# Routed experts of a mixture layer: from dense groups of 16 to a ranking by popularity, with 216 experts in 18 tiles of 12 on 64 token slots

## What is computed

```
h = einsum('btd,pd->btp', x, hasher_w)          # 1024 -> 32
sim = einsum('btp,np->btn', h, keys)            # 256 experts
vals, idx = top_k(sim, 4);  w = softmax(vals)
for k in range(4):
    vd = values_down[idx[..., k]]               # [1024, 32] per row
    vu = values_up[idx[..., k]]                 # [32, 1024] per row
    proj = silu(einsum('btd,btdp->btp', x, vd))
    out += einsum('btp,btpd->btd', proj, vu) * w[..., k:k+1]
return x + out * scale
```

## Time and profile before

| What | us |
|---|---|
| median of three runs | 723.6 |
| span of the profiled execution (first to last instruction) | 720.9 |
| first instruction after the indices of the four experts are known (L1287) | starts at 363.65 |
| one group of 16 experts in the loop | 22.7 |
| end of the last output scaling (L1344) | 718.3 |

### The profile page before, as it was taken

The page is one execution under the profiler, slowest core; times in us unless marked ns, Lnnn a source line. Parts: engine busy times, 40 slices in busy tenths (PEclk is TensorE's granted clock), DMA queues, the critical chain, the costliest instruction groups (busy, mean ns, idle before and its releaser), DMA issues.

```text
span 720.9 us, 9534 instructions
## 1 busy us (share of the span) xinstructions
PE 693.8 (96%) x3308; PEld 544.3 (76%) x3308; DVE 504.1 (70%) x702; ACT 379.9 (53%) x486; POOL 203.2 (28%) x289
## 2 busy tenths in 40 slices
PE   3999999998999999999999999999999999999998
PEld 3877877785555566677878888888888888888886
DVE  5997798599999999677988553464534645356453
ACT  4854989766655656356644534255342543335430
POOL 4038975398489916500500000000000000000000
PEclk9999999999999999999999999999999999999999
DMA  8985332341000006429436536644366444664401
GB/s 307 341 310 221 125 116 88 148 156 78 1 2 1 1 0 243 178 88 340 155 120 241 212 141 218 233 148 181 142 227 233 135 167 163 233 230 127 187 38 60
DMA packets 55177, 114.20 MB, mean 158 GB/s; under 512 B 2245, under 2 KB 35397, under 8 KB 55146
## 3 DMA queue, kind: packets, MB, share of 16 engines
q1 hardware_dynamic: 54538, 112.95, 43.6%
q0 software_dynamic: 160, 0.66, 0.3%
q10 hardware_dynamic: 448, 0.20, 0.1%
HBM read 112.74 MB, written 1.05 MB: 158 GB/s over the span
## 4 chain that ended last, share of the span: by engine, by line
PE 58%; POOL 6%; DVE 5%; issue 5%; ACT 1%; DMA 1%; DVEq 1%; ACTq 0%; POOLq 0%
PE ps L1384 16%; PE ps L1386 16%; PE ps L1385 16%; PE ps L1352 2%; POOL pen L560 2%; POOL oh_src L562 2%; PE ps L1617 2%; POOL pen L567 1%; DVE wlo L870 1%; DVE ps L1057 1%; PE ps L1697 1%; DMA raw<-in_L_gnn_W_on_dram 1%; DVE segmax L1128 1%; PE ps L1678 1%; ACT whi L627 1%
## 5 line engine op out<-in xcount | busy, mean ns | idle before, releaser
L870 DVE TENSOR_TENSOR wlo<-raw,whi 128x2048 fp32r<-128x2048 f32 x99 | 224.4, 2290 | 55.4 <-ACT whi L627 54.7
L627 ACT ACTIVATE whi<-raw 128x2048 fp32r<-128x2048 f32 x104 | 196.3, 1912 | 82.8 <-PE ps L1386 64.8
L1384 PE MATMUL ps<-whi,nT 128*128 128x512 f32 x392 | 157.1, 401 | 0.3 <-ACT act_g L826 0.3
L1386 PE MATMUL ps<-wlo,nT 128*128 128x512 f32 x392 | 153.1, 390 | 0.0
L1385 PE MATMUL ps<-whi,nT 128*128 128x512 f32 x392 | 152.9, 390 | 0.0
L1057 DVE SCALAR_TENSOR_TENSOR ps<-ps,xt 128x1024 f32<-128x1024 f32 x79 | 96.3, 1221 | 1.7 <-PE ps L1410 1.6
L1309 DVE TENSOR_TENSOR gw<-act_g,route 128x512 f32<-128x512 f32 x32 | 20.7, 689 | 105.2 <-ACT act_g L834 105.1
L1384 PE MATMUL ps<-whi,gT_hi 128*128 128x512 f32 x240 | 93.5, 390 | 0.0
L1386 PE MATMUL ps<-wlo,gT_hi 128*128 128x512 f32 x240 | 93.5, 390 | 0.0
L1385 PE MATMUL ps<-whi,gT_lo 128*128 128x512 f32 x240 | 93.4, 389 | 0.0
L1384 PEld LDWEIGHTS ps<-whi,nT 128*128 128x128 f32 x392 | 73.6, 188 | 18.6 <-issue 3.2
(11 more groups left out here) (269 smaller groups left out, 913.4 us busy)
## 6 DMA issues: line engine op xcount, KB each, us to landing
raw<-n_L_ffn_values_down_dram SPq DMA_DIRECT2D x16, 2048.0 KB, 8.2
raw<-in_L_ffn_values_up_dram SPq DMA_DIRECT2D x16, 2048.0 KB, 7.5
raw<-in_L_gnn_W_hh_dram SPq DMA_DIRECT2D x8, 1024.0 KB, 6.1
raw<-in_L_gnn_W_oo_dram SPq DMA_DIRECT2D x8, 1024.0 KB, 6.6
raw<-in_L_gnn_W_ho_dram SPq DMA_DIRECT2D x8, 1024.0 KB, 4.8
raw<-in_L_gnn_W_hn_dram SPq DMA_DIRECT2D x8, 1024.0 KB, 4.8
raw<-in_L_gnn_W_on_dram SPq DMA_DIRECT2D x8, 1024.0 KB, 5.0
xt<-in_x_dram SPq DMA_DIRECT2D x4, 512.0 KB, 7.2
```

What stands on the lines that cost most here:

```text
L627: nc.scalar.activation(half(whi, s, j, down), half(raw, s, j, down), ACT.Copy)\
L870: nc.vector.tensor_tensor(half(wlo, s, j, down), half(raw, s, j, down), half(whi, s, j, down).bitcast(F32), ALU.subtract)\
L1384: nc.tensor.matmul(o, a_hi, b_hi, start=start, stop=False)
L1386: return nc.tensor.matmul(o, a_hi, b_lo, start=False, stop=stop)
```

## The change

Group 0 (experts 0 to 15) stays as it was ("static"). The other 240 experts are ranked by how many tokens chose them. The 24 most chosen ("hot") run dense as before, in 2 groups of 12 (`PER`). The 216 left ("cold") are dealt in turn into 18 tiles (`COLD`) of 12, which run in 9 pairs (`PAIRS`). A tile works on at most 64 tokens (`SLOTS`), those that chose one of its 12 experts: with both parts of x side by side, 64 high and 64 low columns fill the 128 columns of a weight load, and one pass over the high and one over the low part of the matrix gives all products. The rows of x are brought into their slots by matmuls with one-hot matrices (`pick`, by `move_rows`), the routing weights too (`move_weights`), and the results go back to their tokens by matmuls with the turned one-hots (`put`, by `scatter`).

The matrices of a unit (12 experts, down or up, 1.5 MB) are no longer one DMA but 12 of 128 KB, one per expert, at an address that is read from a list of ranks (`by_rank`) into registers of the issuing engine. SP issues the down units, GpSimd the up units. There are three raw buffers of 1.5 MB in a ring (`RAWS`), in which unit n uses buffer n % 3; unit n waits for `lo` of unit n-3 (`raw_free`). A down unit of pair i is number 2+4i+a, an up unit 8+4i+a (the last two 38 and 39), a being 0 or 1.

The loads, as helpers:

```diff
+        def experts(queue, first):
+            return nc.values_load_multi_w_load_instructions(
+                by_rank[0:1, first:first + PER], engines=[queue.engine], min_val=0, max_val=XP - 1,
+                skip_runtime_bounds_check_because="a permutation of the experts, from counted comparisons")[1]
+        def load_down(queue, n, first):
+            down = raw_ring[n % RAWS].rearrange("p (n k) -> p n k", n=PER)
+            for q, e in enumerate(experts(queue, first)):
+                queue.dma_start(down[:, q:q + 1, :], down_v[:, bass.ds(e, 1), :]).then_inc(raw_loaded[n % RAWS], 16)
+        def load_up(queue, n, first):
+            up = raw_ring[n % RAWS].rearrange("p (b d) -> p b d", b=BLK)
+            for q, e in enumerate(experts(queue, first)):
+                at = PD * (q % 4)
+                queue.dma_start(up[at:at + PD, q // 4, :], up_rows[:, bass.ds(e, 1), :].rearrange("w a d -> w (a d)"))\
+                    .then_inc(up_loaded[n % RAWS], 16)
+        def raw_free(queue, n):
+            if n < RAWS:
+                queue.wait_ge(lo_ready[n - 1], 2 * (SLOT_W + 1))
+            else:
+                queue.wait_ge(lo_ready[(n - RAWS) % 2], 2 * turn_of(n - RAWS) + 2)
```

GpSimd's program in this stage (`choose` writes 4 one-hots of 128x64, `write_twice` copies those of a pair, 2 of 128x256; `rows_rest` writes the low part of x, 128x1024):

```diff
+            rows_rest(0)
+            pool.wait_ge(list_ready, 1)
+            raw_free(pool, 2)
+            load_up(pool, 2, 0)
+            pool.wait_ge(taken_ready, 1)
+            choose(0)
+            choose(1)
+            raw_free(pool, 3)
+            load_up(pool, 3, PER)
+            rows_rest(1)
...
+            for pair in range(2, PAIRS):
+                choose(pair)
+            for i in range(PAIRS):
+                write_twice(i)
+                if i:
+                    for a in range(2):
+                        raw_free(pool, up_unit(i - 1, a))
+                        load_up(pool, up_unit(i - 1, a), HOT + (2 * i - 2 + a) * PER)
+            for a in range(2):
+                raw_free(pool, up_unit(PAIRS - 1, a))
+                load_up(pool, up_unit(PAIRS - 1, a), HOT + (2 * PAIRS - 2 + a) * PER)
```

ScalarE's program for pair i (VectorE's has the same order, with `ring_lo`, `add_down`, `cold_weigh`, `sum_lo_part`, `cold_gT_lo` and `x_lo_part` in the places of their partners):

```diff
+                ring_hi(up_unit(i - 1, 0), (0,))
+                send_across(i, 0)
+                ring_hi(up_unit(i - 1, 0), (1,))
+                ring_hi(up_unit(i - 1, 1), (0,))
+                send_across(i, 1)
+                cold_silu(i)
+                sum_hi_part(i - 1, 0, 0)
+                sum_hi_part(i - 1, 0, 1)
+                put_part(i)
+                cold_gT_hi(i)
+                ring_hi(up_unit(i - 1, 1), (1,))
+                ring_hi(after(nxt, 0), (0,))
+                if i < PAIRS - 1:
+                    x_hi_part(i // 2 + 1, 2 * (i % 2))
+                ring_hi(after(nxt, 0), (1,))
+                sum_hi_part(i - 1, 1, 0)
+                sum_hi_part(i - 1, 1, 1)
+                if i < PAIRS - 1:
+                    x_hi_part(i // 2 + 1, 2 * (i % 2) + 1)
+                ring_hi(after(nxt, 1))
```

```diff
+            turn_static()
...
+            up_static()
...
+            hot_down(0)
...
+            hot_turn(0)
+            pe.wait_ge(silu_ready, 2)
+            hot_down(1)
+            pe.wait_ge(gTlo_ready, 2)
+            move_weights(0)
+            hot_up(0)
...
+            hot_turn(1)
...
+            move_rows(0, 0)
+            hot_up(1, lambda b: move_rows(0, b + 1))
+
+            for i in range(PAIRS):
+                cold_down(i, 0)
+                if i >= 2:
+                    scatter(i - 2, 1)
+                cold_down(i, 1)
+                if i:
+                    cold_up(i - 1, 0)
+                else:
+                    move_weights(1)
+                turn_picks(i)
+                cold_turn(i)
+                if i:
+                    scatter(i - 1, 0)
+                if i < PAIRS - 1:
+                    pe.wait_ge(gTlo_ready, 3 + i + 1)
+                    pe.wait_ge(put_ready, i + 1)
+                    move_rows(i // 2 + 1, 2 * (i % 2))
+                if i:
+                    cold_up(i - 1, 1)
+                if i < PAIRS - 1:
+                    move_rows(i // 2 + 1, 2 * (i % 2) + 1)
```

More of the change, by code:

```diff
@@ L83 @@
 GX = 16
-NG = XP // GX
 UNIT = 4096
@@ new lines, in _, with choose @@
+            for t in range(NT):
+                pool.wait_ge(norm_ready, NT + t + 1)
+                nc.gpsimd.tensor_tensor(xt[:, t, :], xt[:, t, :], nf[:, t, :], ALU.add).then_inc(x3_ready, 1)
+            def choose(pair):
+                for j in (2 * pair, 2 * pair + 1):
+                    for t in range(NT):
+                        last = nc.gpsimd.tensor_scalar(pick[:, t, j, :], iota16[:, 1:SLOTS + 1], taken[:, t, j:j + 1], None,
+                                                       ALU.is_equal)
+                last.then_inc(pick_ready, 1)
@@ L856, in _ @@
+            for a in range(2):
+                for h in range(2):
+                    sum_hi_part(PAIRS - 1, a, h)
         @block.vector
@@ new lines, in part_ready, with hot_down @@
+            def part_ready(n, j):
+                pe.wait_ge(lo_ready[n % 2], 2 * turn_of(n) + j + 1)
+            def hot_down(u):
+                for c in range(C):
+                    if c % 4 == 0:
+                        part_ready(u, c // 4)
+                    for t in range(NT):
+                        last = three(bank(4 + t)[:, 0:PERW], nT[:, c, t_hi[t]], nT[:, c, t_lo[t]],
+                                     part_hi[u][:, c, :], part_lo[u][:, c, :], start=c == 0, stop=c == C - 1)
+                    if c % 4 == 3:
+                        last.then_inc(used[u], 1)
@@ new lines, in hot_turn, with hot_up @@
+            def hot_turn(u):
+                pe.wait_ge(gw_ready, 2 + u)
+                for b in range(BLK):
+                    for t in range(NT):
+                        last = transpose(ps[:, 6 * HALF + b * N + t * P:6 * HALF + b * N + (t + 1) * P],
+                                         gw[:, t, b * P:(b + 1) * P])
+                last.then_inc(gT_done, 1)
+            def hot_up(u, between=None):
+                pe.wait_ge(gTlo_ready, 2 + u)
+                for k in range(2 * BLK):
+                    h, b = k // BLK, k % BLK
+                    if b == 0:
+                        part_ready(2 + u, h)
+                    for t in range(NT):
+                        last = three(bank(2 * t + h), hot_hi[:, b, t_hi[t]], hot_lo[:, b, t_hi[t]],
+                                     chunk_hi[u][:, k, :], chunk_lo[u][:, k, :], start=False, stop=False)
+                    if k % BLK == BLK - 1:
+                        last.then_inc(used[u], 1)
+                    if between and k % 2 == 1:
+                        between(k // 2)
@@ new lines, in move_weights @@
+            def move_weights(n):
+                some = range(4 * n, 4 if n == 0 else PAIRS)
+                pe.wait_ge(pick_ready, some.stop)
+                for i in some:
+                    o = bank(7)[:, XP + (i - 4 * n) * 2 * PER:XP + (i - 4 * n + 1) * 2 * PER]
+                    for t in range(NT):
+                        both = route[:, t, FIRST_COLD:XP].rearrange("p (e j) -> p j e", j=COLD)[:, 2 * i:2 * i + 2, :]
+                        last = nc.tensor.matmul(o, pick[:, t, 2 * i:2 * i + 2, :].rearrange("p j s -> p (j s)").bitcast(F32),
+                                                both, start=t == 0, stop=t == NT - 1)
+                last.then_inc(weights_moved, 1)
@@ new lines, in scatter @@
+            def scatter(i, a):
+                pe.wait_ge(put_ready, i + 1)
+                for rows, ready in zip(sums_of(i, a), (sumhi_ready, sumlo_ready)):
+                    for h in range(2):
+                        pe.wait_ge(ready, 4 * i + 2 * a + h + 1)
+                        for t in range(NT):
+                            nc.tensor.matmul(bank(2 * t + h), put[:, i % 2, a, t_hi[t]], rows[:, h * HALF:(h + 1) * HALF],
+                                             start=False, stop=False)
@@ new lines, in _ @@
+            for t in range(NT):
+                for k in range(TOPK):
+                    last = nc.tensor.matmul(bank(4)[:, 0:XP], ones16[:], chosen16[:, t, k, :],
+                                            start=t == 0 and k == 0, stop=t == NT - 1 and k == TOPK - 1)
+            last.then_inc(popular, 1)
+            turn_static()
+            pe.wait_ge(silu_ready, 1)
+            pe.wait_ge(atrank_ready, 1)
+            for b in range(2):
+                last = nc.tensor.matmul(bank(5)[0:1, 0:XP], expert16[:, b:b + 1], at_rank[:, b, :], start=b == 0, stop=b == 1)
@@ new lines, in _ @@
+            scatter(PAIRS - 2, 1)
+            cold_up(PAIRS - 1, 0)
+            pe.wait_ge(put_ready, PAIRS)
+            cold_up(PAIRS - 1, 1)
+            scatter(PAIRS - 1, 0)
+            for h in range(2):
+                for rows, ready in ((last_hi, sumhi_ready), (last_lo, sumlo_ready)):
+                    pe.wait_ge(ready, 4 * PAIRS - 2 + h + 1)
+                    for t in range(NT):
+                        last = nc.tensor.matmul(bank(2 * t + h), put[:, (PAIRS - 1) % 2, 1, t_hi[t]],
```

(3 more changed lines are left out.)

622 lines of the change are left out of this document (489 added, 133 removed).

## The result

| | before | after |
|---|---|---|
| median of 13 runs, us | 724.53 (721.87 to 726.02) | 731.19 (726.09 to 739.07) |
| ratio after / before | | 1.0089, 95% interval 1.0063 to 1.0116 |
| span of the profiled execution, us | 720.9 | 737.4 |

The change makes the kernel 0.9% slower. The forecast was 674, with a range of 612 to 728, and faster. The profiled execution of after is the longest of its 13 runs (739.07, 8 us over the median).

The account below looks back on a forecast made before the run. GpSimd's DMA issues, in a circle of buffer waits, were taken as the new bound: 439 + 7 x (2I + 12.4) + 4I + 14.1, with I = 7.3 per up unit, gave 671.3 us of span, so 674 us; range 612 to 728.

Parts of the forecast that it names:

- start of the first circle: The way through routing and hot groups until unit 5 is split, where the circle starts: at 439 us.
- four units and the end: After the seventh circle: GpSimd issues four units without a wait, 4I, then landing, splits, last products and store, 14.1 us.
- the circle: Cold pairs: buffer freed, GpSimd issues two up units, the last lands, it is split, buffer free again; period 27.0 us.
- The leg behind the landing: In the circle: splitting the second up unit, with the next pair's silu and weights between its halves; 9.4 us.
- L, the landing: In the circle: the wait for the last issued up transfer to land; 3 us, taken between 2.1 and 5.0.
- The issues (0.56): Each of GpSimd's 24 DMA issues per cold pair takes 0.56 us, with bounds of 0.37 and 0.77.
- The 12 register loads: GpSimd's loads of expert addresses in front of each up unit; 0.5 us.
- 2I: GpSimd's time to issue a pair's two up units, I being 12 x 0.56 + 0.5 = 7.3 us each.
- SP at 0.37: SP's issues of the down units take 0.37 us each, 5 us a unit, with slack.
- Quick: Rival, chance 0.25: GpSimd's issues are as cheap as SP's, VectorE's work is the bound, period 21; 627 us.
- Slower: Rival, chance 0.15: GpSimd's issues or register loads queue behind VectorE's `lo`, 2I becomes 24.8; 766 us.
- Clock: Rival, chance 0.10: TensorE's waits slow its matmuls, 17.2 us per cold pair becomes 34.4 and the bound; 726 us.

Follow-up runs that it names:

- e3: The changed kernel with the twelve transfers of an up unit issued in another order of their quarters (0, 2, 1, 3); 732.4 us.
- e4: The changed kernel with both halves of a pair's second up unit split behind the next pair's silu chain, instead of around it; 708.6 us.
- h1: The changed kernel with GpSimd reading the 24 registers of a pair's up units before it waits for the buffer; 719.1 us.
- g2: The changed kernel with each up matrix written to 32 partitions that lie 4 apart, rows still 4 KB; 719.3 us.
- e1: The changed kernel with the up units issued by SP as well, in order of unit numbers, GpSimd issuing nothing; 697.8 us.
- g4: g1 with GpSimd's addition of the input and the graph layer's result moved behind its one-hots; 664.6 us.
- g1: The changed kernel with halves of units on both queues, second up unit split behind the silu chain, up matrices on partitions 4 apart; 665.6 us.
- h3: h2 with SP also fetching the up units of the two hot groups; 659.0 us.
- h2: g1 with each queue's register loads read before it waits for the unit's buffer; 655.7 us.
- g5: The changed kernel with an up unit as one 1.5 MB DMA over 128 partitions, experts in the order of their numbers; 690.5 us.

## Why the prediction was wrong

The span of after, and that of e3's profile, against the prediction's three parts:

| Part | predicted | after | more | e3 | more |
|---|---|---|---|---|---|
| start of the first circle (second half of unit 5 split) | 439 | 455.7 | 16.7 | 450.4 | 11.4 |
| 7 circles | 7 x 27.0 = 189 | 230.7 | 41.7 | 226.6 | 37.6 |
| four units and the end | 43.3 | 51.0 | 7.7 | 50.8 | 7.5 |
| span | 671.3 | 737.4 | 66.1 | 727.8 | 56.5 |

*What bounds it* was right. TensorE isn't the bound, the circle is, with its three legs in the order that was written down, and e4, h1 and g2 each shorten one leg and move the time. The leg behind the landing was 9.5 us for 9.4.

*The step that failed most is L, the landing, 3 us.* It was 8.2 us in the circle read above and 7.6 in the mean of six (7.0 in e3), that is 4.6 of the 6.7 us per circle. The prediction put it between two rows, an unhindered store of 2.1 us and a load of GpSimd's of 5.0 us under load, both single transfers and not the last of 24. And it set the DMA aside as "close to the bound, and not taken for it", with 361 GB/s from the earlier trace rows, a row of transfers over 128 partitions. In after a pair's up units ran beside SP's down units at 234 GB/s, with the down units queued at the same time. A pair's 6.3 MB at that rate are 27 us, as long as the whole predicted circle. g2 shows how much of it the partitions are: 2.5 us of landing in the mean (1.8 against e3), and 12 us of time. The other 5.1 us, still 2.1 more than predicted, remain where the two queues move 342 GB/s; how much of that is plain latency wasn't tried.

*The issues (0.56) were nearly right:* 0.49 busy, 0.57 from start to start, and with the short pauses 14.0 for 13.4 us a circle. *The 12 register loads (0.5 us, from 8 loads of TensorE's) were mis-sized:* 0.84 us, 0.7 a circle more. *The step from the freed buffer to the first issue* was not in the sum: 0.63 us (h1). The whole first leg is 16.4 us for 2I = 14.6. *SP at 0.37 was wrong,* 0.52 and 1 us a unit in front; it cost nothing in after, and was the whole bound in e1.

*The start* was 16.7 us late (11.4 in e3). Timelines of after, VectorE and GpSimd beside each other at 358 us, ScalarE at the first hot unit, VectorE at the third, and TensorE at the routing weights and in the up products of the first hot group:

```profile
358.23 4.48 DVE L1166 TENSOR_TENSOR wlo<-raw,whi 128x2048 fp32r<-128x2048 f32 x1
...
355.80 4.76 POOL L751 TENSOR_TENSOR xt<-xt,nf 128x1024 f32<-128x1024 f32 x2
...
394.52 2.86 ACT L1033 ACTIVATE whi<-raw_third 128x1536 fp32r<-128x1536 f32 x2 [16.69 <-DMA raw_third<-n_L_ffn_values_down_dram]
...
410.26 8.03 DVE L1708 TENSOR_TENSOR wlo<-raw,whi 128x1536 fp32r<-128x1536 f32 x2
...
421.55 2.64 PE L2298 MATMUL ps<-route,pick 128*128 128x24 f32 x16 [1.88 <-POOL pick L756]
...
428.00 0.63 PE L1841 MATMUL ps<-whi,gT_hi 128*128 128x512 f32 x1
428.43 0.63 PE L1842 MATMUL ps<-whi,gT_lo 128*128 128x512 f32 x1
```

The prediction did not count GpSimd's addition, which was moved ahead of the ranking: VectorE's half beside it took 4.48 us instead of 2.27. The first unit landed at 394.5, 16 us after SP began to issue it (13.3 in e3), since GpSimd's and SP's next units shared the DMA at some 240 GB/s; in e1, where GpSimd issues nothing, it took 8.7 us. `lo` was reckoned at 389.7 and ended at 397.8. From 396 to 402 us the granted clock was 0.50 (1.2 GHz), from 422 to 430 0.57, after waits of 6.65 and 1.88 us. The pricing of VectorE beside GpSimd was right in kind and too small: two halves took 8.03 us where 3.4 were reckoned (in e3 these took 3.45, and the weighting before them 3.78 instead of 1.03). Two of these, taken alone, gave nothing back: the addition (g4, tried on g1) and the hot up units (h3, tried on h2).

**The rivals.** *Quick* is out: an issue costs the 0.56 of GpSimd, and VectorE isn't the bound (61%). *Slower* gave the sign and is out as a mechanism: beside VectorE's `lo` at 561.27 the issues stayed at 0.49, as the Trainium skill's rule had it (SBUF — State Buffer, Who interferes with whom), and GpSimd's one-hots did stall (0.43 us at the median of 36, 3.55 at worst). VectorE's timeline of after:

```profile
561.27 1.76 DVE L1708 TENSOR_TENSOR wlo<-raw,whi 128x1536 fp32r<-128x1536 f32 x1 [2.60 <-ACT whi L1033]
```

Right sign, wrong cause. *Clock* came true in part. Between 470 and 640 us the granted clock was 0.85 in the mean, and 0.50 after long waits of TensorE, as in the stretch from 574 us above. So the 1.00 of the earlier trace rows was no evidence for this kernel, and the rule of the Trainium skill (TensorE: Matmul & The Clock Gate, HAM oscillation) was the better guide. But it isn't what costs: TensorE has slack in the circle, except in the start. There, at the half clock, matmuls of 512 columns start 0.43 us apart instead of 0.23 (the two lines at 428 us), and some 11 of these and 11 of 384 columns (0.32 instead of 0.17) ran so; by these rows an estimate is 4 us. No run separated it.

**The expected gain** is found again in the other versions. TensorE's busy time fell from 693.8 to 599.5 us, part of it at half clock; after spends the gain in waits. h2 is 68 us under before.

## What to carry to other kernels

When big loads are cut into pieces, price the pieces as pieces: their issue and the register loads in front of it, on every queue, and the partitions that each one reaches; a rate measured on loads over 128 partitions doesn't hold for 32 neighbouring ones. Price register loads on the engine that makes them. Where two queues and a small ring of buffers are involved, write the circle down (free, issue, land, split, free) and shorten the legs one by one, at first those that cost nothing: what the splitting engines do between landing and release, and what the issuing engine could have read before its wait. A bound that no engine's busy time shows is found by following one buffer once around.

## What the runs showed of the hardware that was not expected

- 128 KB transfers to 32 neighbouring partitions, beside others over 128: 234 GB/s at a DMA share of 1.08; to 32 partitions 4 apart: 342 at 1.02, in a stretch with fewer up units in it. Down units alone: 349.
- A DMA issue with its address in a register costs 0.52 us from start to start on SP and 0.57 on GpSimd; 12 register loads cost GpSimd 0.84 us (h1).
- Beside two 1.5 MB transfers of GpSimd's queue, the last 128 KB of SP's took 9.96 us to land (g5); the median of down transfers in e1, where SP's is the only queue with loads, was 2.2 to 2.3.
- While much is on its way, GpSimd pauses for 2.2 us after eight issues of a unit, for nothing that the profile shows (in after at 591.70 and 702.62). It was not looked into.

```profile
591.70 2.23 POOL L557 DMA_DIRECT2D raw_third<-in_L_ffn_values_up_dram  x4 [2.17 <-issue]
```
